# Decoder layer on one core: four more weight chunks split inside attention, and the last batch taken tile by tile

## What is computed

```python
x = _layernorm(x + attention(x, q, k, v, o))          # causal, 16 heads of 16
x = _layernorm(x + experts_by_token_id(x, itok, ctx)) # 4 experts, ctx[e] as gate, up and down
x = _layernorm(x + top1_moe(x, Wr, br, Wg, Wu, Wd))   # 4 experts, 256 -> 1024 -> 256
```

## Time and profile before

| | us |
|---|---|
| median of 3 runs | 329.6 |
| lowest, highest | 328.85, 330.39 |
| profiled execution | 325.26 |
| its span | 323.4 |
| TensorE busy in it | 248.2 (77%) |
| VectorE busy | 187.7 (58%) |
| ACT busy | 131.5 (41%) |
| mean granted TensorE clock | 0.925 |

### The profile page before, as it was taken

How to read it: one execution, slowest core, us unless ns; L and a number is a source line. 1 busy time by engine, 2 the same in 40 slices (tenths; PEclk the granted TensorE clock), 3 DMA queues, 4 the chain that set the end, 5 groups by cost and what they waited for, 6 DMA issues and landing times.

```text
span 323.4 us, 5887 instructions
## 1 busy us (share of the span) xinstructions
PE 248.2 (77%) x1999; PEld 164.0 (51%) x2000; DVE 187.7 (58%) x422; ACT 131.5 (41%) x218; POOL 72.4 (22%) x124
## 2 busy tenths in 40 slices
PE   4885788877787774366888537489999999999990
PEld 3454555545554442124677532135666656666570
DVE  3868777676696646652587759023544455454541
ACT  4451757476566774124567410033223223333220
POOL 8300000000050502540233358300222011222222
PEclk9999999999999997775899956599999999999997
DMA  6999162422252660728500002240000000000000
GB/s 213 329 295 292 27 253 65 134 65 67 64 150 84 163 197 1 212 82 261 211 3 0 1 13 93 63 126 21 16 18 2 1 12 16 16 16 16 9 11 3
DMA packets 17415, 29.29 MB, mean 91 GB/s; under 512 B 2092, under 2 KB 12910, under 8 KB 17392
## 3 DMA queue, kind: packets, MB, share of 16 engines
q1 hardware_dynamic: 15952, 25.81, 26.9%
q0 software_dynamic: 1440, 3.17, 2.7%
HBM read 19.69 MB, written 10.03 MB: 92 GB/s over the span
## 4 chain that ended last, share of the span: by engine, by line
PE 55%; DVE 16%; issue 10%; DMA 6%; POOL 5%; ACT 5%; SPq 2%; POOLq 0%; ACTq 0%; DVEq 0%
PE ps L1098 35%; PE ps L1412 3%; DVE arena L842 3%; PE ps L1219 2%; PE ps L1169 2%; POOL sorted L447 2%; DMA arena<-Wf 2%; ACT wf_hi L476 2%; PE ps L1104 2%; DMA arena<-arena 2%; POOL sorted L420 2%; DVE wf_lo L682 1%; SPq L333 1%; PE ps L1165 1%; DMA ring<-wqkvT 1%
## 5 line engine op out<-in xcount | busy, mean ns | idle before, releaser
L1098 PE MATMUL ps<-wf_hi,arena 128*128 x336 | 81.9, 329 | 2.6 <-DVE arena L1026 1.6
L1098 PE MATMUL ps<-wf_lo,arena 128*128 x168 | 55.2, 328 | 0.0
L1098 PEld LDWEIGHTS ps<-wf_hi,arena 128*128 128x128 f16 x336 | 32.8, 98 | 26.6 <-issue 6.5
L635 ACT ACTIVATE arena<-ps 128x512 f32<-128x512 f32 x22 | 13.2, 598 | 64.9 <-PE ps L1098 64.9
L1026 DVE SCALAR_TENSOR_TENSOR arena<-ps,arena 128x512 f32<-128x512 f32 x22 | 15.2, 692 | 24.4 <-ACT arena L635 13.5
L1104 PE MATMUL ps<-wf_hi,ones 128*128 128x512 f16 x51 | 19.0, 549 | 11.9 <-issue 6.8
L412 POOL TENSOR_SCALAR veps<-mv 128x2 f32<-128x2 f32 x4 | 2.6, 640 | 103.4 <-DVE mv L890 103.4
L682 DVE SCALAR_TENSOR_TENSOR wf_lo<-ring,wf_hi 128x1024 f16<-128x1024 f32 x17 | 20.4, 1218 | 7.2 <-ACT wf_hi L476 7.2
L1098 PE MATMUL ps<-xT_hi,arena 128*128 x88 | 20.3, 296 | 5.3 <-DVE arena L986 4.6
L1098 PEld LDWEIGHTS ps<-wf_lo,arena 128*128 128x128 f16 x168 | 16.4, 98 | 9.4
L1219 PE MATMUL ps<-arena 128*32 128x256 f32 (+1 forms) x256 | 13.7, 331 | 8.9 <-DVE arena L862 5.5
(11 more groups left out here) (203 smaller groups left out, 525.2 us busy)
## 6 DMA issues: line engine op xcount, KB each, us to landing
ring<-Wf SPq DMA_DIRECT2D x17, 512.0 KB, 4.0
sorted<-fill SPq DMA_DIRECT2D x1, 4515.0 KB, 22.7
arena<-Wf SPq DMA_DIRECT2D x7, 512.0 KB, 7.4
arena<-sorted SPq DMA_DIRECT2D x22, 129.0 KB, 2.1
sorted<-fill SPq DMA_DIRECT2D x1, 1419.0 KB, 7.6
ring<-xT SPq DMA_DIRECT2D x4, 256.0 KB, 5.2
X<-x_tok SPq DMA_DIRECT2D x1, 1024.0 KB, 7.8
ring<-ctxT SPq DMA_DIRECT2D x2, 512.0 KB, 3.8
```

The source lines that it names most:

```text
L635: a.activation(sg[:, half * 512:(half + 1) * 512], ps[:, 2 * half, :], ACT.Silu, scale=1 / W_SCALE).then_inc(sg3, 1)
L1098: last = t.matmul(dst, xs(k), ws(k), start=(k == 0 and m == 0), stop=(k == nk - 1 and m == 2))
```

## The change

In words:

- `ATT_CHUNKS` goes from 15 to 19. Steps 9, 10, 11, 13 and 14 split two chunks on ACT and on VectorE, step 15 none, the others one as before.
- `stats1` of batch 2 moves from behind the loop into step 15, between `residual(2)` and `outputs(14)`.
- Batch 3 is handled tile by tile, each tile with banks of its own (`LAST_T` = 7, 6 for the transposes, `LAST_O` = 4, 5 for the projection): two transposes, high half, low half, projection, residual, statistics and reciprocal deviation of one tile, then of the other, interleaved.
- Chunks 19 and 20, the only ones left to split ahead of stage 2, get their low halves only after POOL has issued the last scatters (`scat2_sent`, set by a small memset behind them).
- Dummy matmuls are added on TensorE: 2 ahead of the last batch's transposes, 4 ahead of its projection, 8 ahead of the 16 that were there, and 8 behind a wait for all scatters (`scat2`).

```diff
-        ATT_CHUNKS = NCH - LATE - RING
+        ATT_CHUNKS = NCH - LATE
+        def chunks_at(step):
+            return 0 if step in (0, STEPS - 1) else 2 if step in (9, 10, 11, 13, 14) else 1
...
-                while n < min(step + RING, NCH - LATE):
+                used += chunks_at(step)
+                while n < min(used + RING, ATT_CHUNKS):
                     load(n)
...
-            pool.wait_ge(mv1, NT)
-            inv_std(mv[:, :, 1], TB, rs1)
+            for j in range(TB):
+                tt = NT - TB + j
+                pool.wait_ge(mv1, tt + 1)
+                link(g.tensor_scalar(veps[:, j:j + 1], mv[:, j, 1:2], EPS, None, ALU.add))
+                g.tensor_tensor(rstd[:, j:j + 1], veps[:, j:j + 1], minus_half[:, 0:1], ALU.pow).then_inc(rs1, 1)
             scatter2(B - 1)
+            g.memset(veps[:, :], 0.0).then_inc(scat2_sent, 1)
...
-            o_hi(B - 1)
+            for j in range(TB):
+                act.wait_ge(oT_last, j + 1)
+                a.activation(OT_hi[:, j], ps[:, LAST_T[j], 0:D].rearrange("p (k t) -> p k t", k=NK),
+                             ACT.Copy).then_inc(oT_hi_last, 1)
...
                         residual(b - 1)
-                        if b < B - 1:
-                            stats1(b - 1)
+                        stats1(b - 1)
...
-            stats1(B - 2)
             norm1(B - 2)
-            o_lo(B - 1)
-            split_lo(n)
-            n += 1
-            residual(B - 1)
-            stats1(B - 1)
-            norm1(B - 1)
+            for j in range(TB):
+                dve.wait_ge(oT_hi_last, j + 1)
+                if j == 0:
+                    dve.wait_ge(wo_rdy, TB * (B - 1))
+                v.tensor_tensor(OT_lo[:, j], ps[:, LAST_T[j], 0:D].rearrange("p (k t) -> p k t", k=NK), OT_hi[:, j],
+                                ALU.subtract).then_inc(oT_lo_last, 1)
...
+            last_residual(0)
+            last_mean(0)
+            last_residual(1)
+            last_mean(1)
+            for j in range(TB):
+                tt = NT - TB + j
+                dve.wait_ge(rs1, B + j)
+                v.tensor_scalar(X1[:, tt, 0:D], X1[:, tt, 0:D], mv[:, j, 0:1], rstd[:, j:j + 1],
+                                ALU.subtract, ALU.mult).then_inc(x1_rdy, 1)
+            dve.wait_ge(scat2_sent, 1)
             while n < NCH - LAST:
                 split_lo(n)
...
-            out_T(B - 1)
-            out_project(B - 1)
+            keep_warm(2, wf_hi[:, 0:512], bank=0)
+            for j in range(TB):
+                if j == 0:
+                    pe.wait_ge(o_norm, STEPS)
+                    pe.wait_ge(res1, NT - TB)
+                for k in range(NK):
+                    last = t.transpose(ps[:, LAST_T[j], k * P:(k + 1) * P], On[:, j, k * P:(k + 1) * P], identF[:, :])
+                last.then_inc(oT_last, 1)
+            keep_warm(4, wf_hi[:, 0:512], bank=0)
+            for j in range(TB):
+                pe.wait_ge(oT_lo_last, j + 1)
+                three(ps[:, LAST_O[j], 0:D], lambda k: OT_hi[:, j, k], lambda k: OT_lo[:, j, k],
+                      lambda k: wo_hi[:, k], lambda k: wo_lo[:, k], NK).then_inc(wo_rdy, 1)
 
             pe.wait_ge(tile_rdy, 1)
             experts = [pe.value_load(tile_i[0:1, 0, i:i + 1], min_val=0, max_val=E - 1) for i in range(NS)]
+            keep_warm(WARM_GAP, wf_hi[:, 0:512], bank=0)
             pe.wait_ge(res1, NT)
             pe.wait_ge(x1_rdy, NT)
             keep_warm(2 * WARM_GAP, wf_hi[:, 0:512])
+            pe.wait_ge(scat2, 16 * NT)
+            keep_warm(WARM_GAP, wf_hi[:, 0:512])
```

More of the change, by code:

```diff
@@ L31 @@
 SLOT = 64
+LAST_T, LAST_O = (7, 6), (4, 5)
 HEAD = 32
@@ L211, in build @@
         lg_sb, ex_rdy, w_rdy, row_rdy = (sem(n) for n in ("lg_sb", "ex_rdy", "w_rdy", "row_rdy"))
+        oT_last, oT_hi_last, oT_lo_last, scat2_sent = (sem(n) for n in ("oT_last", "oT_hi_last", "oT_lo_last", "scat2_sent"))
         endT, end_hi, end_lo = sem("endT"), sem("end_hi"), sem("end_lo")
@@ L256, in build @@
         xTv_lo = xT_lo[:, :].rearrange("p (k t) -> p k t", k=NK)
-        ATT_CHUNKS = NCH - LATE - RING
+        ATT_CHUNKS = NCH - LATE
+        assert ATT_CHUNKS <= NCTX + (E - 1) * (EW // CH)
+        def chunks_at(step):
+            return 0 if step in (0, STEPS - 1) else 2 if step in (9, 10, 11, 13, 14) else 1
+        assert sum(chunks_at(step) for step in range(STEPS)) == ATT_CHUNKS
         CTX_AT = 8
@@ L563, in _ @@
                     q_odds(stacked_at(step))
-                if step >= 1 and n < ATT_CHUNKS:
+                for _ in range(chunks_at(step)):
                     split_hi(n)
@@ L937, in _ @@
                     stacks(stacked_at(step))
-                if 1 <= step < STEPS - 1 and n < ATT_CHUNKS:
+                for _ in range(chunks_at(step)):
                     split_lo(n)
@@ L946, in _, with last_residual, last_mean @@
             outputs(STEPS - 1)
-            stats1(B - 2)
             norm1(B - 2)
-            o_lo(B - 1)
-            split_lo(n)
-            n += 1
-            residual(B - 1)
-            stats1(B - 1)
-            norm1(B - 1)
+            for j in range(TB):
[4 more added lines that the diff above has]
+                                ALU.subtract).then_inc(oT_lo_last, 1)
+            def last_residual(j):
+                tt = NT - TB + j
+                dve.wait_ge(wo_rdy, tt + 1)
+                v.scalar_tensor_tensor(out=X1[:, tt, 0:D], in0=ps[:, LAST_O[j], 0:D], scalar=1 / W_SCALE,
+                                       in1=X1[:, tt, 0:D], op0=ALU.mult, op1=ALU.add).then_inc(res1, 1)
+                dve.wait_ge(res1, tt + 1)
+                v.bn_stats(st[:, j, :], X1[:, tt, 0:D]).then_inc(bn1, 1)
+            def last_mean(j):
+                tt = NT - TB + j
+                dve.wait_ge(bn1, tt + 1)
+                v.bn_aggr(mv[:, j, :], st[:, j, :]).then_inc(mv1, 1)
+            last_residual(0)
[3 more added lines that the diff above has]
+            for j in range(TB):
+                tt = NT - TB + j
+                dve.wait_ge(rs1, B + j)
+                v.tensor_scalar(X1[:, tt, 0:D], X1[:, tt, 0:D], mv[:, j, 0:1], rstd[:, j:j + 1],
+                                ALU.subtract, ALU.mult).then_inc(x1_rdy, 1)
+            dve.wait_ge(scat2_sent, 1)
             while n < NCH - LAST:
```

2 lines of the change are left out of this document (1 added, 1 removed).

## The result

The changed kernel is slower: 333.51 us median of 20 runs (329.1 to 335.35) beside 327.25 (324.59 to 330.39) for 20 of the kernel before. The ratio is 1.0174 (95% interval 1.0146 to 1.0202), that is +5.7 us. The sign was forecast as the likeliest and 333.51 lies in the range, but the size was not: I had +2.1. That it lies in the range is luck in part. The range was laid around a median of three runs, 329.6, and that of twenty is 327.25; as a change, the range went from -2.2 to +4.6, and +5.7 lies outside it. The profiled execution took 332.14 us.

What follows compares the result with a forecast made beforehand. VectorE's chain was taken to bound attention's steps 9 to 14; afterwards TensorE's loads and dummies decide. Last `outputs` 124.99 + 4.7 + 0.95 + 0.8 = 131.4, stage 2 150.8, `a_hi` 157.7 (+2.1): 329.6 + 2.1 = 331.7 us, range 327.4 to 334.2.

Steps and rivals of the forecast that it cites:

- Added splits, +4.7: Attention, steps 9 to 14: four more chunks on VectorE's queue delay the last `outputs` by 4.7 us, bounds 2.4 to 5.8.
- Statistics of batch 2, +0.95: Attention, step 15: batch 2's statistics, moved ahead of `outputs(14)`, add 0.95 us on the path.
- The clock inside attention: Attention, steps 9 to 11: TensorE's clock may fall, slowing one projection on the path by 0 to 1.5 us, taken as 0.8.
- rival D: Clock falls twice in attention, or stays low through the 32 dummies (13.7 us): +4.5 us, 334.1, chance 0.12.
- Tile by tile, 2.3: Last batch: from the last `outputs` to the end of the low half takes 2.3 us, before 3.36.
- Register loads 7.6, dummies 9.4: TensorE between last projection and stage 2: eleven register loads take 7.6 us, then 32 dummies 9.4; stage 2 starts at 150.8.
- Stage 2, 6.9 to `a_hi` of tile 3: Stage 2: first transposes to `a_hi` of tile 3 take 6.9 us, before 10.1, without the weight wait and at full clock.
- Scatters about 1.0 each: POOL's last two scatters: about 1.0 us each with splits held, gaining 5.5 us on their own path.
- Rival C: Last scatters: one stays slow by 4 us despite held splits, something else being the cause; +3.4 us, 333.0, chance 0.08.
- Rivals A and B: A: room in VectorE's queue, middle -2.2 us, chance 0.20; B: transfers, not dummies, set the pace, middle -0.8, chance 0.10.
- From the trace to the median: Whole kernel: the +2.1 us summed against the profiled execution is added to the runs' median 329.6, giving 331.7.

## Why the prediction was right or wrong

I go by its own steps. The changed kernel's profiled execution was already 0.70 us late ahead of step 9 (its split 8 at 97.00, before at 96.30), which no step of mine covers.

- **Added splits, +4.7.** Right: 2.26 by `outputs(9)`, 1.12 by `outputs(10)` beyond what the clock cost, 1.13 by `outputs(12)`, nothing in step 14; 4.5 in all.
- **Statistics of batch 2, +0.95.** Right: `outputs(14)` moved by 0.9 more than the step before it.
- **The clock inside attention, 0 to +1.5, taken as 0.8.** This is the term that failed. It fell twice and each fall cost 1.5 us on the path (residual of step 11, `outputs(13)`): 3.0 in all, and the run that fills those gaps gives 3.1 back. The step that failed is that I looked at one place, steps 9 to 11, and put the second fall into rival D with its 12%, as if it were another case. It was the same mechanism: `values(13)` waited for `outputs(12)`, behind the two splits of step 13, and just before it for ACT's copy, behind ACT's two halves. The clock also fell in step 15 and cost 0.2 there. I had priced a projection only; `values` on the path (0.86 to 1.51) falls with it. The last `outputs` ended at 134.33, not 131.4: 2.2 for the clock, 0.7 for the late execution.
- **Tile by tile, 2.3.** Right, 2.04.
- **Register loads 7.6, dummies 9.4.** Right in kind and nearly in size: 8.2 and 9.67. Stage 2 started 17.7 us behind the low half, where I had 17.1.
- **Stage 2, 6.9 to `a_hi` of tile 3.** Right, 7.08, and split 21 didn't wait. 161.14 against my 157.7: the 3.4 are the 2.2 and 0.7 above, and 0.5 left over from the smaller terms (0.6 more for loads and dummies, 0.2 more in stage 2, 0.3 less for tile by tile).
- **Scatters about 1.0 each.** Right, 1.09 and 0.97, and right that the gain would be real and unused: the second scatter started 4.2 behind the projection's end in place of 9.35, and TensorE reached tile 0 only at 154, without a wait.
- **Rival C, the scatter still slow.** It fell. I had taken from the Trainium skill, "SBUF — State Buffer", section "Who interferes with whom", that an instruction of two SBUF inputs leaves descriptor generation free, by which a hold would win nothing. Added to the kernel before, the hold alone won 3.2 us and brought 5.01 to 1.07. The same section of the Trainium skill also says "Issue order, not op shape, decides who blocks". The starts agree with that sentence only in part: 0.25 ahead of a split took 1.09, 0.05 behind 2.14, 0.56 behind 5.01, but 0.80 behind (197.83 against 197.03) took 1.25. That splits lost no time beside the scatter that came first is not what a lock held by the scatter would show. And my reading that "a queue of splits without a gap shuts POOL out" rests on one scatter; the two of 1.97 and 1.98 in the same trace speak against it as a rule.
- **Rival D.** As a change from the kernel before, +5.7 lies nearer its +4.5 than the forecast's +2.1, and its first half came true: the clock fell twice in attention. Its second half, 32 dummies wholly at the low clock, didn't (9.67, not 13.7).
- **Rivals A and B.** Neither came. A's room in VectorE's queue exists, ahead of the residuals as I had noted, and the kernel with splits there shows it; the change doesn't use it.
- **From the trace to the median.** `a_hi` of tile 3 moved by 5.55 and the span by 6.9: 0.6 more came in the rest of stage 2 and 0.7 at the start of the last sub-layer. The runs' ratio gives 5.7. The 0.70 of the start is that execution's own; whether the others are is not shown, I did not trace them.

By parts, from the ratios and in this order: the hold added to the kernel before, -3.2; the other parts but the chunks, from 0.9902 to 0.9989, +2.8; the chunks on top, +6.0. Of the +2.8 the added dummies make +2.4 if the four runs without them are right, and the tile-by-tile handling and the moved statistics the rest, which is within what these ratios can tell. Another order gives other parts: with tile-by-tile handling the hold is worth nothing, and in the kernel before without the hold the chunks cost 3.5.

## What to carry to other kernels

Before adding work to an engine that a pipelined loop waits for, look at each place where TensorE then waits: if the wait grows, price the clock's fall there, in every such place, on each matmul of the path. Put such work where the engine idles for someone else, even if the program has to name those steps. And ask what stands in TensorE's own order between the event that was made earlier and the work that was to profit; register loads and dummies queued there can hold the whole gain.

## What the runs showed of the hardware

- In the changed kernel the clock fell behind a wait of 2.15 us and behind waits of 0.86 and 1.87 in a row, and held behind one of 3.18 at 113.95; in the kernel without the added dummies it fell at that same place, behind 2.70. The length of a single wait does not tell whether the clock falls.
- Eleven register loads on TensorE's sequencer took 8.2 us behind the projection; spread over attention's steps they let the dummies start right behind it.
- An indirect scatter of 0.97 to 1.09 us grew to 5.01 beside VectorE's queued splits when it began 0.56 behind the first, to 2.14 when 0.05 behind, to 1.25 when 0.80 behind, and not at all when it began 0.25 ahead. Each is one execution.
- With three chunk loads in flight rather than two, the wait for the last scatter's rows ended 5.3 us behind its start (133.61 to 138.91) and not 3.2 (135.80 to 138.98).
